# Attention: running sums in 64x64 quadrants of the array, denominators from their own sums of k, their inverses in PSUM

## The chip, the cores and the metric

The kernel runs on one core of a Trainium2 chip. The metric is the device time of one execution in microseconds: 632.59 us is the median of three runs of the kernel before (632.16 to 632.62).

## What is computed

One decoder layer on x of 128 sequences of 64 tokens with 128 features, in float32: causal linear attention with 16 heads of 8 features, a cross attention by autocorrelation, and a mixture of 8 experts. The change touches the linear attention alone:

```python
q = fm(xn @ wq + bq); k = fm(xn @ wk + bk); v = xn @ wv + bv     # fm(a) = a + 1 if a > 0 else exp(a)
# per sequence and head, over the tokens t in order:
S = S + k[:, None] * v[None, :]          # 8 x 8
z = z + k                                # 8
out_t = (q @ S) / ((q . z) + 1e-6)
x = x + out @ wo + bo
```

## The kernel before, in words

The 8192 tokens are 64 tiles of 128 (two sequences of 64 each), in 16 groups of 4 tiles. The attention, and the Gram matrices of the cross attention that follows it, run as a software pipeline of slots, one slot a group: `slot(n)` does stage a0 (statistics and normalisation) of group n+2, a1 (transpose, projection, features, outer products) of group n+1, b (running sums, product with q, sum over d) of group n, c (division, output projection, residual) of group n-1, and d (second normalisation, Gram products) of group n-2. Each engine has its own `slot` function, and the order of its instructions there is the order in which it executes them; semaphores tie the engines. Slots 2 to 13 are in a loop of two slots an iteration, the others are written out.

In one slot, for each tile k of four:

- TensorE projects the normalised, transposed rows to q, k, v (`project`, one 384-column product into bank 1). ScalarE takes the three out (L647, L648, L650, L653); GpSimd adds the two parts of the feature map (L534) and makes the outer product of v and k (L542). v has a ninth column of ones in each head (`v9`, D1 = 9), so that the outer product holds k itself as a ninth row: 16 x 9 x 8 = 1152 columns.
- TensorE multiplies it by a 128x128 block-triangular matrix of ones, `tri_s` (`running_sums`): the running sums over the tokens of each sequence. 1152 columns don't fit one PSUM bank, so there are three products, of 6, 5 and 5 heads, into banks 2, 3 and 4. VectorE multiplies each piece by q (`times_q`, L896), and one reduction sums over d (`sum_heads`, L905) into `nd`, which holds numerators and denominators. As each piece has its own semaphore count, TensorE may refill a bank as soon as its piece of the last tile is multiplied.

In the slot after, ScalarE adds the epsilon to the denominators (L658), VectorE inverts them (`inverses`, L930), and multiplies (`quotients`, L935: both inputs in SBUF). TensorE transposes the quotients (L1333), ScalarE copies them out (L693), TensorE projects them with a bias product, VectorE adds them to X (`add_attention`, L943) and takes the statistics of the sum (L869, L877).

A float32 product is two instructions in the trace, each with its own weight load. All products go through line 1329, all transposes of four tiles through line 1333. The array's order in a slot is: transposes of xh; sums of tile 1; projection 0; the product of `wkk` with the context; projection 1; transposes of the quotients; sums 2; output projection; projection 2; transposes of xh2; sums 3; projection 3; sums of tile 0 of the next group; the Gram products, which are eight 64-column products into the upper and the lower half of the output partitions.

Of the kernel before, what the change touches and what calls it, by code (L numbers as in the profile page):

```python
# [13 lines left out]
P = 128  # L14
B, L, E, H = 128, 64, 128, 16
D = E // H
D1 = D + 1
T = B * L
NT = T // P
GT = 4  # L20
# [33 lines left out]
HEADS = [(0, 6), (6, 11), (11, 16)]  # L54
# [13 lines left out]
def build(nc, x, ctx_t, ctx_r, wqkv_p, b_all, wo, wq2, wk2, wv2t, wo2, bq2, bk2, bv2, scale, w_router, w_experts,  # L68
          tri, stri, ident, iota, dest, walk, place, late_in, out):
    with ExitStack() as ctx:  # L70
        def sb(name, shape, dt=F32):
            return ctx.enter_context(nc.sbuf_tensor(name, shape, dt))

        def sem(name):
            return ctx.enter_context(nc.semaphore(name))

        def sems(name, n):
# [52 lines left out]
        v9 = [sb(f"v9_{i}", [P, H, D1]) for i in range(2)]  # L130
        qk = [sb(f"qk{i}", [P, GT, 2 * E]) for i in range(2)]

        shared = sb("shared", [P, GT * H * D1 * D])
        bias_f, bias_r, bias_a, bias_b = (shared[0:3, i * NBIAS:(i + 1) * NBIAS] for i in range(4))
        b_wide = shared[:, 4 * NBIAS:4 * NBIAS + 3 * E]
        outer = [shared[:, i * H * D1 * D:(i + 1) * H * D1 * D].rearrange("p (h e d) -> p h e d", h=H, e=D1)
                 for i in range(GT)]
        R = sb("R", [P, H, D1, D])
        nd = [sb(f"nd{i}", [P, GT, H, D1]) for i in range(2)]
        den, rden = sb("den", [P, GT * H]), sb("rden", [P, GT * H])  # L140
# [81 lines left out]
        is_tile = [halves(R[:].rearrange("p h e d -> p (h e d)")[:, i * PAIRS * NT:(i + 1) * PAIRS * NT], PAIRS, NT, 2)  # L222
                   for i in range(2)]
        row_t = R[:].rearrange("p h e d -> p (h e d)")[:, NSORT * NT:NSORT * NT + P]
# [13 lines left out]
        bank = [ctx.enter_context(nc.psum_tensor(f"bank{i}", [P, 512], F32)) for i in range(8)]  # L238

# [16 lines left out]
        b_run, b_mul, b_red = sem("b_run"), sem("b_mul"), sem("b_red")  # L256

# [38 lines left out]
        def settle(eng):  # L296


            eng.sem_inc(settled, 1)
# [200 lines left out]
        def _(pool):  # L500
# [5 lines left out]
            for k in range(2):  # L506
                pool.memset(v9[k][:], 1.0).then_inc(setup, 1)
# [5 lines left out]
            pool.wait_ge(setup, 5)  # L513
# [14 lines left out]
            def features(g, p, r, k):  # L528
                t = GT * g + k

                pool.wait_ge(a_ex, t + 1)
                need(pool, b_mul, 3 * (t - 2 * GT) + 3)
                need(pool, a_outer, t - 2 * GT + 1)
                nc.gpsimd.tensor_tensor(qk[p][:, k, :], ex[k % 2][:], rl[k % 2][:], ALU.add).then_inc(a_f, 1)  # L534

            def outer_product(g, p, r, k):
                t = GT * g + k
                pool.wait_ge(a_f, t + 1)
                pool.wait_ge(a_pev, 3 * t + 3)
                need(pool, b_run, 3 * (t - GT) + 3)  # L540
                kk = qk[p][:, k, E:2 * E].rearrange("p (h d) -> p h d", h=H)
                nc.gpsimd.tensor_tensor(  # L542
                    outer[k], v9[k % 2][:].unsqueeze(3).broadcast_to([P, H, D1, D]),
                    kk.unsqueeze(2).broadcast_to([P, H, D1, D]), ALU.mult).then_inc(a_outer, 1)
# [91 lines left out]
        def _(act):  # L636
# [5 lines left out]
            def a_evac_proj(g, p, r, k):  # L642
                t = GT * g + k
                act.wait_ge(a_proj, t + 1)
                need(act, a_f, t - 1)

                nc.scalar.activation(ex[k % 2][:], bank[1][:, 0:2 * E], ACT.Relu, scale=-1.0).then_inc(a_pev, 1)  # L647
                nc.scalar.activation(rl[k % 2][:], bank[1][:, 0:2 * E], ACT.Relu).then_inc(a_pev, 1)  # L648
                need(act, a_outer, t - 1)
                nc.scalar.activation(v9[k % 2][:, :, 0:D], bank[1][:, 2 * E:3 * E].rearrange("p (h d) -> p h d", h=H),  # L650
                                     ACT.Copy).then_inc(a_pev, 1)
                act.wait_ge(a_pev, 3 * t + 1)
                nc.scalar.activation(ex[k % 2][:], ex[k % 2][:], ACT.Exp, scale=-1.0).then_inc(a_ex, 1)  # L653

            def denominators(g, p, r):
                act.wait_ge(b_red, GT * g + GT)
                need(act, c_rden, g)
                nc.scalar.activation(den[:], nd[p][:, :, :, D].rearrange("p t h -> p (t h)"), ACT.Copy, bias=ATT_EPS).then_inc(c_den, 1)  # L658
# [15 lines left out]
            def slot(n, i):  # L674
                a0, a1, c, d = (stage(n, i, s) for s in (2, 1, -1, -2))
# [8 lines left out]
                if c:  # L684
                    denominators(*c)
# [20 lines left out]
                if a1:  # L706
                    a_evac_proj(*a1, 2)
                if a0:
# [118 lines left out]
        def _(dve):  # L827
# [59 lines left out]
            def times_q(g, p, r, k, pieces):  # L887
                t = GT * g + k
                if pieces[0] == 0:
                    need(dve, b_red, t)  # L890
                for c in pieces:
                    lo, hi = HEADS[c]
                    n_h = hi - lo
                    dve.wait_ge(b_run, 3 * t + c + 1)
                    qq = qk[p][:, k, lo * D:hi * D].rearrange("p (h d) -> p h d", h=n_h)
                    nc.vector.tensor_tensor(  # L896
                        R[:, lo:hi], bank[2 + c][:, 0:n_h * D1 * D].rearrange("p (h e d) -> p h e d", h=n_h, e=D1),
                        qq.unsqueeze(2).broadcast_to([P, n_h, D1, D]), ALU.mult).then_inc(b_mul, 1)

            def sum_heads(g, p, r, k):  # L900
                t = GT * g + k
                dve.wait_ge(b_mul, 3 * t + 3)
                if k == 0:
                    need(dve, c_on, g - 1)
                nc.vector.tensor_reduce(nd[p][:, k], R[:], AX.X, ALU.add).then_inc(b_red, 1)  # L905

# [20 lines left out]
            def inverses(g, p, r):  # L927
                dve.wait_ge(c_den, g + 1)
                need(dve, c_on, g)
                nc.vector.reciprocal(rden[:], den[:]).then_inc(c_rden, 1)  # L930

            def quotients(g, p, r):
                dve.wait_ge(c_rden, g + 1)
                need(dve, c_tr, g)
                nc.vector.tensor_tensor(  # L935
                    on[:].rearrange("p t (h d) -> p (t h) d", h=H), nd[p][:, :, :, 0:D].rearrange("p t h d -> p (t h) d"),
                    rden[:].unsqueeze(2).broadcast_to([P, GT * H, D]), ALU.mult).then_inc(c_on, 1)
# [8 lines left out]
            def slot(n, i):  # L946
                a0, a1, b, c = (stage(n, i, s) for s in (2, 1, 0, -1))
                if b:
                    times_q(*b, 0, (0, 1, 2))
                if b:  # L950
                    sum_heads(*b, 0)
                if c:
                    inverses(*c)
                if b:
                    times_q(*b, 1, (0,))
                if c:
                    quotients(*c)
                if b:
                    times_q(*b, 1, (1, 2))
# [4 lines left out]
                if b:  # L964
                    sum_heads(*b, 1)
                if a0:
                    moments(a0[0], a0[1], st_a, a_st, mv_a, a_mv, a_nb, GT)
# [9 lines left out]
                if b:  # L977
                    times_q(*b, 2, (0, 1, 2))
# [7 lines left out]
                if b:  # L986
                    times_q(*b, 3, (0,))
                if c:
                    moments(c[0], c[1], st_c, c_st, mv_c, c_mv, c_nb, GT)
                if b:  # L990
                    times_q(*b, 3, (1, 2))
                    sum_heads(*b, 3)
# [14 lines left out]
            dve.wait_ge(setup, 12)  # L1007
# [319 lines left out]
        def _(pe):  # L1327
# [7 lines left out]

            def running_sums(g, p, r, k):
                t = GT * g + k
                pe.wait_ge(a_outer, t + 1)
                for c, (lo, hi) in enumerate(HEADS):
                    need(pe, b_mul, 3 * (t - 1) + c + 1)  # L1340
                    mm(bank[2 + c][:, 0:(hi - lo) * D1 * D], tri_s[:], outer[k][:, lo:hi].rearrange("p h e d -> p (h e d)")
                       ).then_inc(b_run, 1)

            def project(g, p, r, k):
                t = GT * g + k
                if k == 0:
                    pe.wait_ge(a_xT, g + 1)
                need(pe, a_pev, 3 * t)
                mm(bank[1][:, 0:3 * E], xT[:, k * P:(k + 1) * P], wqkv[:]).then_inc(a_proj, 1)
# [6 lines left out]
            def slot(n, i):  # L1356
# [15 lines left out]
                if b:  # L1372
                    running_sums(*b, 1)
                if a1:
# [12 lines left out]
                if i is None and n == NG:  # L1387
                    pe.wait_ge(b_mul, 3 * NT)
                    keep_warm(2, 10)
                if c:  # L1390
                    pe.wait_ge(c_on, c[0] + 1)
                    transposes(bank[5], on).then_inc(c_tr, 1)
# [47 lines left out]
            pe.wait_ge(setup, 5)  # L1440
# [11 lines left out]
            pe.wait_ge(b_mul, 3 * NT)  # L1452
# [64 lines left out]
            pe.wait_ge(setup, 11)  # L1517
# [196 lines left out]
```

## Time and profile before

| | us |
|---|---|
| median of three runs | 632.59 |
| span of the profiled execution | 631.7 |
| what its run took beyond the span, about | 0.9 |
| first product with q | 21.78 |
| first product with q of group 15 | 252.61 |
| Gram products of group 13 | 263.90 |
| TensorE, VectorE, GpSimd, ScalarE busy | 575.6, 517.9, 427.0, 420.2 |

The attention is the stretch from the first product with q to about 278 us. The second part of the transfer of the Gram diagonals waits for the Gram products of group 13, and everything after it waits for that transfer, so the time at which slot 15 does these products is the end of this stage. Read it slot by slot: a slot is the time from one group's first product with q to the next group's.

### The profile page before, as it was taken

The numbers are of one execution on the slowest core, as the hardware profiler recorded it, in microseconds if no ns is written. First come the engines' busy times: TensorE is split into PE (matmuls) and PEld (weight loads), VectorE is DVE, ScalarE is ACT, GpSimd is POOL, SyncE is SP. The second block draws the span as 40 slices with busy tenths as digits, with TensorE's granted clock in tenths as the row PEclk, the third lists the DMA queues.
The fourth block names the chain that finished last, engine by engine and source line by source line (L and its number), as shares of the span: only waits on it lengthen the run. The fifth ranks groups of instructions, "written<-read, shape, count | busy, mean of one in ns | idle before, by whom it ended". The sixth has DMA issues, their size and how long they took to land.

```text
span 631.7 us, 15833 instructions
## 1 busy us (share of the span) xinstructions
PE 575.6 (91%) x3838; PEld 442.8 (70%) x3839; DVE 517.9 (82%) x1602; ACT 420.2 (67%) x1188; POOL 427.0 (68%) x461
## 2 busy tenths in 40 slices
PE   3899999999999999968799877999999999999993
PEld 1455555555555555545689644799999999989993
DVE  5599999999999999983678888566877887877883
ACT  3557777877787777351788512345788888878882
POOL 2899989998999899310877600765467666757762
PEclk9999999999999999999999968899999999999998
DMA  5610111111161111283477551221012111111110
GB/s 147 184 51 0 35 33 35 34 33 33 33 100 33 34 33 34 66 119 90 119 208 202 113 113 29 53 51 46 27 49 54 48 47 47 51 38 51 51 44 23
DMA packets 49973, 40.92 MB, mean 65 GB/s; under 512 B 21971, under 2 KB 40278, under 8 KB 49926
## 3 DMA queue, kind: packets, MB, share of 16 engines
q1 hardware_dynamic: 44150, 29.61, 19.0%
q0 software_dynamic: 4960, 10.49, 6.4%
q8 instruction: 20, 0.33, 0.2%
q10 hardware_dynamic: 816, 0.26, 0.2%
q14 instruction: 27, 0.22, 0.1%
HBM read 27.47 MB, written 12.88 MB: 64 GB/s over the span
## 4 chain that ended last, share of the span: by engine, by line
PE 63%; ACT 12%; DVE 12%; issue 6%; DMA 4%; POOL 1%; DVEq 0%; ACTq 0%; SPq 0%; POOLq 0%
PE bank L1329 57%; PE bank L1333 4%; ACT xh L671 3%; ACT xs L773 2%; PE bank L1568 2%; DMA w_s<-gram_d 1%; DVE on L935 1%; ACT ex L647 1%; ACT nb_c L668 1%; DVE mean_early L1037 1%; DMA circ<-prob_d 1%; PE bank L1492 1%; ACT rl L648 1%; ACT xrT L759 1%; ACT ex L653 1%
## 5 line engine op out<-in xcount | busy, mean ns | idle before, releaser
L542 POOL TENSOR_TENSOR shared<-v,qk 128x1152 f32<-128x1152 f32 x64 | 142.8, 2231 | 2.8
L1329 PE MATMUL bank<-shared,tri_s 128*128 128x360 f32 (+1 forms) x384 | 137.2, 494 | 0.7 <-DVE R L896 0.7
L609 POOL DMA_INDIRECT shared<-xs_d,row_u x91 | 87.8, 964 | 62.2 <-DVE row_u L1227 31.6
L896 DVE TENSOR_TENSOR R<-bank,qk 128x360 f32<-128x360 f32 (+1 forms) x192 | 96.2, 540 | 8.6 <-PE bank L1329 6.7
L1329 PEld LDWEIGHTS bank<-shared,tri_s 128*128 128x128 f32 x384 | 69.8, 192 | 44.9 <-issue 20.4
L616 POOL DMA_INDIRECT out_x<-shared x64 | 63.6, 993 | 48.4 <-DVE shared L1299 21.8
L905 DVE TENSOR_REDUCE nd<-R 128x144 f32<-128x1152 f32 x64 | 86.1, 1346 | 1.6
L1329 PE MATMUL bank<-w_s,hid 128*128 (+1 forms) x620 | 82.3, 276 | 0.1
L1329 PEld LDWEIGHTS bank<-w_s,hid 128*128 128x128 f32 x620 | 75.5, 192 | 0.6 <-issue 0.3
L812 ACT ACTIVATE shared<-bank 128x256 f32<-128x256 f32 x155 | 59.4, 384 | 21.9 <-PE bank L1329 16.2
L1320 DVE TENSOR_TENSOR hid<-bank,shared 128x256 f32<-128x256 f32 x155 | 61.4, 422 | 10.0 <-ACT shared L812 9.8
L1329 PE MATMUL bank<-shared,ct 128*128 128x128 f32 x512 | 67.8, 275 | 0.0
L1329 PE MATMUL bank<-shared,u 128*128 128x128 f32 x512 | 67.6, 275 | 0.0
L1329 PE MATMUL bank<-wqkv,xT 128*128 128x384 f32 x128 | 56.7, 526 | 6.9 <-ACT v L650 4.6
L1329 PEld LDWEIGHTS bank<-shared,ct 128*128 128x128 f32 x512 | 62.2, 192 | 0.3 <-issue 0.2
L1329 PEld LDWEIGHTS bank<-shared,u 128*128 128x128 f32 x512 | 62.3, 192 | 0.0
L802 ACT ACTIVATE shared<-bank,scale_s 128x128 f32<-128x128 f32 (+1 forms) x78 | 30.1, 386 | 41.1 <-PE bank L1568 41.1
L534 POOL TENSOR_TENSOR qk<-ex,rl 128x256 f32<-128x256 f32 x64 | 48.0, 751 | 9.7 <-ACT ex L653 9.6
L647 ACT ACTIVATE ex<-bank 128x256 f32<-128x256 f32 x64 | 24.1, 376 | 36.2 <-PE bank L1329 36.2
L1329 PEld LDWEIGHTS bank<-wqkv,xT 128*128 128x128 f32 x128 | 22.5, 198 | 29.7 <-ACT v L650 21.6
L806 ACT ACTIVATE ct<-w_s 128x512 f32 x64 | 39.7, 620 | 0.1
L1329 PE MATMUL bank<-ones 128*128 128x512 bf16 x128 | 36.0, 423 | 0.0
(247 smaller groups left out, 1138.4 us busy)
## 6 DMA issues: line engine op xcount, KB each, us to landing
xs_d<-xs SPq DMA_DIRECT2D x16, 270.0 KB, 4.7
X<-in_x SPq DMA_DIRECT2D x16, 256.0 KB, 2.8
ct<-in_ctx_t SPq DMA_DIRECT2D x16, 256.0 KB, 2.8
ct<-in_ctx_r SPq DMA_DIRECT2D x16, 256.0 KB, 3.6
gram_d<-gd SPq DMA_DIRECT2D x14, 256.0 KB, 2.4
w_s<-in_w_experts SPq DMA_DIRECT2D x8, 384.0 KB, 4.0
circ<-prob_d SPq DMA_DIRECT2D x30, 64.0 KB, 2.7
shared<-xs_d,row_u POOLq DMA_INDIRECT x91, 2.6
```

The source lines that it names most:

```text
L534: nc.gpsimd.tensor_tensor(qk[p][:, k, :], ex[k % 2][:], rl[k % 2][:], ALU.add).then_inc(a_f, 1)
L542: nc.gpsimd.tensor_tensor(outer[k], v9[k % 2][:].unsqueeze(3).broadcast_to([P, H, D1, D]), kk.unsqueeze(2).broadcast_to([P, H, D1, D]), AL ...
L609: nc.gpsimd.indirect_dma_start(xg[q], None, xs_d[:, :], bass.IndirectOffsetOnAxis(ap=rows, axis=0)).then_inc(xg_in[q], 16)
L616: nc.gpsimd.indirect_dma_start(out[:, :], bass.IndirectOffsetOnAxis(ap=xg[(NXI + j) % NX][:, DEST:DEST + 1].bitcast(U32), axis=0), yg[q], ...
L647: nc.scalar.activation(ex[k % 2][:], bank[1][:, 0:2 * E], ACT.Relu, scale=-1.0).then_inc(a_pev, 1)
L802: nc.scalar.activation(xgT[p][:, cols], bank[0][:, cols], ACT.Copy, scale=scale_s[:, 0:1]).then_inc(x_xT, 1)
L806: nc.scalar.activation(w_tile[n % 2][0], w_s[:, dyn(held[0] * W_E, 2 * HID)], ACT.Copy).then_inc(x_wa, 1)
L812: nc.scalar.activation(silu[p][h], bank[1 + 2 * p + h][:, HID:2 * HID], ACT.Silu).then_inc(x_silu, 2 // len(items_of(i, up[0])))
L896: nc.vector.tensor_tensor(R[:, lo:hi], bank[2 + c][:, 0:n_h * D1 * D].rearrange("p (h e d) -> p h e d", h=n_h, e=D1), qq.unsqueeze(2).broa ...
L905: nc.vector.tensor_reduce(nd[p][:, k], R[:], AX.X, ALU.add).then_inc(b_red, 1)
L1320: nc.vector.tensor_tensor(hid[p][h][:], bank[1 + 2 * p + h][:, 0:HID], silu[p][h], ALU.mult).then_inc(x_h, 2 // len(items_of(i, j)))
L1329: return nc.tensor.matmul(o, l, r, start=start, stop=stop, skip_group_check=True)
```

## The change

- The ninth column goes: the outer product has 1024 columns (`v8`, `outer`), the running sums fill exactly two banks (`run`, banks 2 and 3), the product with q is one instruction over both, and the reduction gives the 128 numerators alone (`num`).
- `running_sums` becomes four products of 64 rows, 64 output partitions and 512 columns, one for each quadrant of the array: rows of sequence b and head half c give partitions of half c in bank b. So the results lie with the head half in the partition index.
- To have q in that layout, `project` does k and v as one 256-column product and q as four products of 64 output partitions and 64 columns.
- The denominators have a path of their own, once a group: `key_sums`, four products of 64 output partitions and 256 columns (tri_s by the four tiles' k) into bank 4, after the sums of tile 1; `key_dots` times q and `sum_dots` over d on VectorE around the second tile; ScalarE adds the epsilon after the third tile's features; `inverses` comes before the last `sum_heads` of the same slot and writes into bank 4.
- `quotients` comes right after the first product with q of the next slot, with its second input in PSUM.
- `turn_quotients` replaces the four transposes by sixteen products of 64 rows by 64 columns with the identity, on the two diagonal quadrants.
- One semaphore count a tile in place of three; two memsets at the start go.

The core of the diff:

```diff
-            def running_sums(g, p, r, k):
-                for c, (lo, hi) in enumerate(HEADS):
-                    need(pe, b_mul, 3 * (t - 1) + c + 1)
-                    mm(bank[2 + c][:, 0:(hi - lo) * D1 * D], tri_s[:], outer[k][:, lo:hi].rearrange("p h e d -> p (h e d)")
-                       ).then_inc(b_run, 1)
+                need(pe, b_mul, t)
+                settle(pe)
+                for b in range(2):
+                    for c in range(2):
+                        own = slice(b * L, b * L + L)
+                        last = mm(run[c * L:c * L + L, b * 512:b * 512 + 512], tri_s[own, own], outer[k][own, c * 512:c * 512 + 512])
+                last.then_inc(b_run, 1)
+            def turn_quotients():
+                settle(pe)
+                for k in range(GT):
+                    for b in range(2):
+                        for c in range(2):
+                            own = slice(c * HALF, c * HALF + HALF)
+                            last = mm(bank[5][own, k * P + b * HALF:k * P + b * HALF + HALF],
+                                      on[own, k, b * HALF:b * HALF + HALF], id_s[own, own])
+            def key_sums(g, p, r):
+                pe.wait_ge(a_f, GT * g + GT)
+                need(pe, c_on, g)
+                for b in range(2):
+                    for c in range(2):
+                        last = mm(bank[4][c * L:c * L + L, b * GT * HALF:(b + 1) * GT * HALF], tri_s[:, b * L:b * L + L],
+                                  qk[p][:, :, E + c * HALF:E + c * HALF + HALF])
             def project(g, p, r, k):
-                mm(bank[1][:, 0:3 * E], xT[:, k * P:(k + 1) * P], wqkv[:]).then_inc(a_proj, 1)
+                mm(bank[1][:, E:3 * E], xT[:, k * P:(k + 1) * P], wqkv[:, E:3 * E])
+                for b in range(2):
+                    for c in range(2):
+                        last = mm(bank[1][c * L:c * L + L, b * HALF:b * HALF + HALF], xT[:, k * P + b * L:k * P + b * L + L],
+                                  wqkv[:, c * HALF:c * HALF + HALF])
...
+            def times_q(g, p, r, k):
+                need(dve, b_red, t)
+                dve.wait_ge(b_run, t + 1)
+                nc.vector.tensor_tensor(
+                    R[:, 0:D * E].rearrange("p (h e d) -> p h e d", h=H, e=D),
+                    run[:].rearrange("p (h e d) -> p h e d", h=H, e=D),
+                    qq.unsqueeze(2).broadcast_to([P, H, D, D]), ALU.mult).then_inc(b_mul, 1)
+            def key_dots(g, p, r):
+                dve.wait_ge(b_keys, g + 1)
+                nc.vector.tensor_tensor(
+                    zq[:].rearrange("p (k b x) -> p b k x", k=GT, b=2), bank[4][:].rearrange("p (b k x) -> p b k x", b=2, k=GT),
+                    qk[p][:, :, 0:E].rearrange("p k (b x) -> p b k x", b=2), ALU.mult).then_inc(b_dots, 1)
+            def sum_dots(g, p, r):
+                nc.vector.tensor_reduce(den[:], zq[:].rearrange("p (x d) -> p x d", d=D), AX.X, ALU.add).then_inc(b_dots, 1)
```

In VectorE's slot the order before is: `times_q` 0 (three pieces), `sum_heads` 0, `inverses` of group n-1, first piece of `times_q` 1, `quotients` of n-1, its other pieces, statistics of a0, `sum_heads` 1, its moments, `times_q` 2, `add_attention`, `sum_heads` 2, statistics of c, `times_q` 3 around the moments of c, `sum_heads` 3. After: `times_q` 0, `quotients` of n-1, `sum_heads` 0, `times_q` 1, `key_dots`, statistics of a0, `sum_heads` 1, `sum_dots`, moments, `times_q` 2, `add_attention`, `sum_heads` 2, statistics of c, `times_q` 3, moments of c, `inverses` of n, `sum_heads` 3.

## Rows read from the trace of the kernel before

**Rows 1.** The page: busy time of each engine, and the granted clock over the span.
```profile
PE 575.6 (91%) x3838; PEld 442.8 (70%) x3839; DVE 517.9 (82%) x1602; ACT 420.2 (67%) x1188; POOL 427.0 (68%) x461
...
PEclk9999999999999999999999968899999999999998
```

**Rows 2.** Chain of waits, 100 to 160 us: start, us, what.
```profile
123.78 5.13 PE bank L1329 x30
```

**Rows 3.** Timeline of VectorE, 128 to 144 us: start, us, instruction, idle before.
```profile
128.35 1.49 DVE L896 TENSOR_TENSOR R<-bank,qk 128x432 f32<-128x432 f32 x3
129.87 1.35 DVE L905 TENSOR_REDUCE nd<-R 128x144 f32<-128x1152 f32 x1
131.14 0.54 DVE L930 RECIPROCAL rden<-den 128x64 f32<-128x64 f32 x1
...
132.06 0.68 DVE L935 TENSOR_TENSOR on<-nd,rden 128x512 f32<-128x512 f32 x1
...
133.54 0.86 DVE L869 BATCH_NORM_STATS2 st_a<-X 128x6 f32 x4
134.32 1.33 DVE L905 TENSOR_REDUCE nd<-R 128x144 f32<-128x1152 f32 x1
135.57 0.37 DVE L877 BATCH_NORM_AGGREGATE mv_a<-st_a 128x2 f32<-128x6 f32 x4
...
137.71 0.69 DVE L943 TENSOR_TENSOR X<-X,bank 128x512 f32 x1 [0.32 <-PE bank L1329]
...
142.12 1.35 DVE L905 TENSOR_REDUCE nd<-R 128x144 f32<-128x1152 f32 x1
143.60 1.49 DVE L896 TENSOR_TENSOR R<-bank,qk 128x432 f32<-128x432 f32 x3
```

**Rows 4.** Timeline of TensorE, 126 to 135 us.
```profile
126.19 2.10 PE L1329 MATMUL bank<-shared,tri_s 128*128 128x432 f32 x6
128.22 0.69 PE L1329 MATMUL bank<-x2T,k2T 128*64 128x64 f32 x16
128.84 0.66 PE L1333 MATMUL bank<-id_s,xh 128*128 128x128 f32 x4
129.33 2.10 PE L1329 MATMUL bank<-shared,tri_s 128*128 128x432 f32 x6
131.27 0.81 PE L1329 MATMUL bank<-wqkv,xT 128*128 128x384 f32 x2
...
133.07 0.91 PE L1329 MATMUL bank<-wqkv,xT 128*128 128x384 f32 x2
133.82 0.60 PE L1333 MATMUL bank<-id_s,on 128*128 128x128 f32 x4
```

**Rows 5.** Single products of two kinds, 100 to 200 us: ns min/median/max.
```profile
L1333 PE MATMUL bank<-id_s,xh x48: 272/273/329, 107.8 to 191.6; 128*128 128x128 f32 x48
...
L1329 PE MATMUL bank<-x2T,k2T x96: 222/222/271, 113.0 to 191.0; 128*64 128x64 f32 x96
```

**Rows 6.** Timeline of ScalarE, 132 to 139 us.
```profile
132.19 0.38 ACT L647 ACTIVATE ex<-bank 128x256 f32<-128x256 f32 x1 [1.76 <-PE bank L1329]
...
134.46 0.60 ACT L693 ACTIVATE oT<-bank 128x512 f32<-128x512 f32 x1 [1.14 <-PE bank L1333]
...
136.69 1.65 ACT L671 ACTIVATE xh<-X,nb_c,rs_c 128x128 f32 x4
```

**Rows 7.** The quotients (ns min/median/max of 16), and an outer product beside one.
```profile
L935 DVE TENSOR_TENSOR on<-nd,rden x16: 677/679/2592, 40.3 to 268.2; 128x512 f32<-128x512 f32 x16
...
132.11 2.66 POOL L542 TENSOR_TENSOR shared<-v,qk 128x1152 f32<-128x1152 f32 x1
```

**Rows 8.** Timeline of all engines: first and last slot of the running sums.
```profile
21.78 0.61 DVE L896 TENSOR_TENSOR R<-bank,qk 128x432 f32<-128x432 f32 x1 [4.52 <-PE bank L1329]
...
252.61 1.49 DVE L896 TENSOR_TENSOR R<-bank,qk 128x432 f32<-128x432 f32 x3
...
263.90 0.69 PE L1329 MATMUL bank<-x2T,k2T 128*64 128x64 f32 x16
```

More of the change, by code:

```diff
@@ L53 @@
 PITCH = L * (2 * L + 1)
-HEADS = [(0, 6), (6, 11), (11, 16)]
+HALF = E // 2
 def need(eng, sem, count):
@@ L129, in build @@
         ex, rl = [sb(f"ex{i}", [P, 2 * E]) for i in range(2)], [sb(f"rl{i}", [P, 2 * E]) for i in range(2)]
-        v9 = [sb(f"v9_{i}", [P, H, D1]) for i in range(2)]
+        v8 = [sb(f"v8_{i}", [P, E]) for i in range(2)]
         qk = [sb(f"qk{i}", [P, GT, 2 * E]) for i in range(2)]
-        shared = sb("shared", [P, GT * H * D1 * D])
+        shared = sb("shared", [P, 9 * GT * E])
         bias_f, bias_r, bias_a, bias_b = (shared[0:3, i * NBIAS:(i + 1) * NBIAS] for i in range(4))
         b_wide = shared[:, 4 * NBIAS:4 * NBIAS + 3 * E]
[L136 to L140, printed above, removed]
+        outer = [shared[:, i * D * E:(i + 1) * D * E] for i in range(GT)]
+        R = sb("R", [P, (D + 1) * E])
+        num = [sb(f"num{i}", [P, GT, E]) for i in range(2)]
+        zq = sb("zq", [P, GT * E])
+        den = sb("den", [P, GT * H])
         on = sb("on", [P, GT, E])
@@ L236, in build, with psum @@
         y0 = sb("y0", [P, E])
-        bank = [ctx.enter_context(nc.psum_tensor(f"bank{i}", [P, 512], F32)) for i in range(8)]
+        def psum(name, banks=1):
+            return ctx.enter_context(nc.psum_tensor(name, [P, banks * 512], F32))
+        bank = [psum("bank0"), psum("bank1")]
+        run = psum("run", 2)
+        bank += [run[:, i * 512:(i + 1) * 512] for i in range(2)] + [psum(f"bank{i}") for i in range(4, 8)]
+        rden = bank[4][:, 0:GT * H]
         settled = sem("settled")
@@ L531, in features @@
                 pool.wait_ge(a_ex, t + 1)
-                need(pool, b_mul, 3 * (t - 2 * GT) + 3)
+                need(pool, b_mul, t - 2 * GT + 1)
+                need(pool, b_dots, 2 * (g - 1) - 1)
                 need(pool, a_outer, t - 2 * GT + 1)
@@ L539, in outer_product @@
                 pool.wait_ge(a_pev, 3 * t + 3)
-                need(pool, b_run, 3 * (t - GT) + 3)
+                need(pool, b_run, t - GT + 1)
                 kk = qk[p][:, k, E:2 * E].rearrange("p (h d) -> p h d", h=H)
+                vv = v8[k % 2][:].rearrange("p (h e) -> p h e", h=H)
                 nc.gpsimd.tensor_tensor(
-                    outer[k], v9[k % 2][:].unsqueeze(3).broadcast_to([P, H, D1, D]),
-                    kk.unsqueeze(2).broadcast_to([P, H, D1, D]), ALU.mult).then_inc(a_outer, 1)
+                    outer[k].rearrange("p (h e d) -> p h e d", h=H, e=D), vv.unsqueeze(3).broadcast_to([P, H, D, D]),
+                    kk.unsqueeze(2).broadcast_to([P, H, D, D]), ALU.mult).then_inc(a_outer, 1)
             def slot(n, i):
@@ L674, in slot @@
             def slot(n, i):
-                a0, a1, c, d = (stage(n, i, s) for s in (2, 1, -1, -2))
+                a0, a1, b, c, d = (stage(n, i, s) for s in (2, 1, 0, -1, -2))
                 if i is None and n == 1:
@@ L1391, in slot @@
                     pe.wait_ge(c_on, c[0] + 1)
-                    transposes(bank[5], on).then_inc(c_tr, 1)
+                    turn_quotients().then_inc(c_tr, 1)
                 if i is None and n == NG:
```

81 lines of the change are left out of this document (36 added, 45 removed).

## The prediction

> **What bounds the kernel now.** The page comes first: TensorE is busy for 91% of the span at a granted clock of 0.9 or more nearly everywhere, so most of the kernel is the array's [rows 1]. The change works only in the attention, 21.78 to 263.90 us [rows 8], so what counts is how long a slot lasts there. Fifteen slots, from 21.78 to 252.61, take 230.8 us, 15.39 each; an undisturbed one takes 15.25, from 128.35 to 143.60 [rows 3, 8]. Some are longer because of the quotients: the median is 0.68 us, the longest 2.59 [rows 7]. Beside one of them the outer product on GpSimd took 2.66.
>
> Inside a slot no single engine is the bound. VectorE's line is nearly gapless (0.32 us before L943, 0.13 before the next slot [rows 3]). The chain of waits shows runs such as 5.13 us of TensorE [rows 2]; the timelines show how they continue: sums 1, projection 0, ScalarE's copies, projection 1, transposes of the quotients, ScalarE's copy of them, its copies of projection 1, the second normalisation, transposes of xh2 [rows 4, 6]. So the slot is a ring through TensorE and ScalarE, 15.25 us long, and VectorE's own work is just shorter. A change that lightens each engine still has to shorten the longest ring; that is where I work it out.
>
> **How to read TensorE's rows.** Four transposes take 0.60 us and one takes 0.273 [rows 4, 5], so they start 0.109 apart: 0.85 ns a column for each instruction of a product, and 0.164 us of tail that the next one doesn't wait for. The sums of a tile, 1152 columns in two instructions each, are 1.96; the row gives 2.10 - 0.164 = 1.94.
>
> **Quadrants.** The trace before has one tiled shape, the Gram products: sixteen instructions of 64 columns would be 0.87 us one after another; they took 0.69, less 0.164 and 0.05 of slow start 0.47 [rows 4, 5]. So two run at a time in the two column halves. No row shows two row halves together. The bounds of a tile's sums (eight instructions of 512 columns, 0.435 each) are 0.88 us, four at a time, 1.75, two at a time, and 3.5, one by one. I take 0.88, as the Gram rows are at the full rate for their halves: 1.06 less a tile than now. k's sums are eight instructions of 256 columns, two at a time: 0.87 a group. q's projection is 0.23 a tile and the other 256 columns 0.43, together 0.66 against 0.64. The turned quotients are 32 instructions of 64 columns, 0.92 at two at a time against 0.44 now.
>
> **Changing shape.** The sums before the Gram products end streaming at 126.19 + 2.10 - 0.164 = 128.13; the first Gram instruction starts at 128.22 and takes 0.05 longer than the others: 0.14 us lost. On the way back streaming ends at 128.74, the first transpose starts at 128.84 and takes 0.055 longer: 0.155 lost [rows 4, 5]. Between full-size products nothing is lost. I take 0.15 for each change of shape. Before there are two in a slot; after there are sixteen (around each tile's sums, around the q half of each projection, around k's sums, the turned quotients and the Gram products). TensorE's sum in a slot falls by 4 x 1.06 = 4.2, and grows by 0.87 + 0.1 + 0.5 + 14 x 0.15 = 3.6. So the array gains 0.6 us a slot, not four.
>
> The Trainium skill (TensorEngine Tiling (Array Packing), Key Properties) says that changing the tiling mode drains the array, and that changing the tile within a mode doesn't. The trace agrees for full size against column halves; no row here shows quadrants against column halves. By the rule that is a change too; if it were none, two of the six changes in the ring below would go and the result be 0.3 us a slot, some 4 us in all, lower.
>
> **VectorE.** Three products with q take 1.49 us and VectorE's 512-element product from PSUM 0.69 [rows 3]: 1.04 ns an element and 0.15 fixed, 1.22 for 1024 in one. The reduction goes from 1.35 to 1.21. That is 0.41 less a tile, 1.6 a slot. Added are a product of 512 (0.69, next start after 0.61) and a reduction of 512 (0.68, 0.60): 1.2. The inversion keeps its 0.54 (0.46 to the next start), wherever it stands. The quotients keep 0.68 and lose their long cases, as their second input is no longer in SBUF; today's long slots cost 0.14 a slot over the quiet ones. That gain is real, but only where this ring is the bound. Summed in the new order, each from its start to the next start (product with q 1.14, quotients 0.60, reduction 1.13, or 1.34 where a product with q follows it, statistics 0.78, moments 0.29): 14.5 us. By VectorE alone a slot would be 0.7 shorter. GpSimd's outer product shrinks by a ninth, some 0.2 of 2.2 us; it is not in the ring, as it has more than 3 us to spare before the sums that read it. ScalarE's epsilon only moves (0.3), behind the copies of projection 2, before the first normalisation of group n+2, which the next transposes need only 3 us later.
>
> **The new ring.** Two waits get coarser. The sums of tile k now need the whole product with q of tile k-1 (before: its first piece), and the product with q needs the whole sums. So VectorE enters the ring. From the start of the transposes of xh2: 0.50 for them; 0.15 change; sums 3 0.88; 0.22 until VectorE starts (128.13 to 128.35 [rows 3, 4]); product with q 1.14, moments 0.29, inversion 0.46, reduction 1.21 and 0.13 until the next product with q, 3.23; product with q of tile 0 and 0.10 to the array, 1.32; sums 1 0.88; change and k's sums 1.02; change and k, v 0.58; change and q 0.38; ScalarE's copies, 1.27 from the end of projection 0 at 131.91 to the effective start of projection 1 at 133.18 [rows 4, 6] (the context product lies beside this); k, v 0.43; change and q 0.38; change and turned quotients 1.07; and 4.13 from the end of today's transposes at 134.26 to the transposes of xh2 at 138.39 (ScalarE's copy of the quotients, its four copies of projection 1, and the normalisation that ends at 138.34 [rows 6]; the next sums and the output projection lie beside this). Sum 16.44 us. What waits in it: behind the transposes of xh2 stand sums 3, projection 3 and sums 0, and for sums 3 VectorE waits 0.9 us at its fourth product with q. A smaller wait of 0.8 arises at its third, since between sums 1 and sums 2 the array now has five changes of shape.
>
> **The sum.** Slot 0 has neither division nor Gram products; VectorE's 11.9 us and waits make 13.1 (before 14.8). Slot 1 has the division but no second normalisation: 14.5 + 0.8 + 0.1 for `add_attention` = 15.4. Thirteen slots of 16.44 are 213.7. Together 242.2 against 230.8: +11.4. The first product with q needs all the sums of tile 0: +0.3. Slot 15 has no projections; by the same terms its Gram products come 10.1 us after its start, now 11.3: -1.2. In all +10.5. What follows begins with a transfer that waits for those Gram products, and moves with them. The execution's span 631.7 becomes 642.2; with 0.9 beyond the span, which is also how the profiled run stands to the median 632.59, 643 us. The two memsets at the start lie under the first loads: nothing.
>
> **Rivals.**
> - *Faster: VectorE is the ring.* If the array's changes of shape cost little where instructions wait anyway, and the two waits on VectorE are hidden, a slot is VectorE's 14.5 + 0.1. For: it is today's nearly gapless line. Against: 1.8 us of the ring sum have to vanish. 13.1 + 14 x 14.65 = 218.2, -12.6 + 0.3 - 1.2: 619 us. It decides from where the ring falls under 15.2.
> - *Near no change.* The six changes of the ring cost nothing but the ring stands: 16.44 - 0.9 = 15.54, 13 x 0.9 = 11.7 us less than forecast: 631 us.
> - *Slower still: sums two at a time.* The two instructions of one product follow each other in one quadrant; if the second holds up the next quadrant, a tile's sums are 1.75 and the ring 18.2. 13 x 1.75 and 2 for the first slots: 667 us. One by one it would be 3.5 a tile and some 712.
> - *Slower: the turned quotients one at a time*, 1.84 in place of 0.92, 14 times: 656 us. The mechanism is that the two diagonal quadrants have different row halves and write one bank. The Trainium skill (TensorEngine Tiling (Array Packing), Gotcha 1: PSUM Pressure) says that different row tiles can't access one PSUM bank at the same time. No run here shows it.
>
> **Chances.** Forecast and what lies near it (slots of 15.9 to 16.9, 636 to 650) 0.44; faster 0.21; near no change 0.13, of which 0.04 faster, 0.06 within 0.2%, 0.03 slower; two at a time or worse 0.12; turned quotients 0.10. A measurement of this kernel tells 0.2%, 1.3 us, from no change. Faster 0.25, same 0.06, slower 0.69. The range that holds 8 in 10 reaches from the faster case to the two-at-a-time case: 618 to 667; the likeliest alone is 636 to 650.
>
> **What would show it.** Right: slots of about 16.4 us with VectorE idle before its third and fourth product with q, released by L1329; 0.15 of idle weight loads at each change of shape; a tile's eight instructions within 0.9 us; all sixteen quotients at 0.68. Wrong: no idle time on VectorE (faster); the eight instructions over 1.7 us; a granted clock under 0.9 within the attention, as TensorE's share of a slot falls to about 13.8 of 16.4 us (which I count with nothing, since by the ring it never stands still for longer than about 1.2 us).

## The result, and the profile after

The changed kernel takes 646.54 us (median of 4 runs, 646.11 to 647.40); the kernel before took 632.54 beside it (4 runs). The ratio is 1.0217 [1.0202, 1.0231]: 14.0 us slower. The profiled execution has a span of 645.6 and a time of 647.4. Forecast were 643 us, 618 to 667.

The page of the changed kernel: span, then busy time of each engine, the granted clock in 40 slices, and who holds the chain that ends last [rows 1].

```profile
span 645.6 us, 18065 instructions
...
PE 562.5 (87%) x5054; PEld 419.2 (65%) x5055; DVE 504.7 (78%) x1506; ACT 417.8 (65%) x1188; POOL 410.0 (64%) x459
...
PEclk9999999999999999999999977899999999999997
...
PE 59%; ACT 14%; DVE 11%; issue 8%; DMA 3%; POOL 2%; ACTq 0%; DVEq 0%; POOLq 0%; SPq 0%
```

Every engine is lighter (TensorE by 13 us, VectorE by 13, GpSimd by 17, ScalarE by 2) and the kernel is longer. TensorE's granted clock is as before (in both traces it is on record as 1.00 from 25 to 366 us, so in nearly all of the attention). That is what a ring does: each engine has slack, and the way round them has grown.

The same stretch of two engines, one slot. Columns: start, us, instruction, idle before and what ended it. VectorE first [rows 3]:

```profile
132.45 1.23 DVE L897 TENSOR_TENSOR R<-run,qk 128x1024 f32<-128x1024 f32 x1 [0.97 <-PE run L1342]
133.59 0.37 DVE L882 BATCH_NORM_AGGREGATE mv_c<-st_c 128x2 f32<-128x6 f32 x4
133.87 0.53 DVE L945 RECIPROCAL bank<-den 128x64 f32<-128x64 f32 x1
134.31 1.17 DVE L907 TENSOR_REDUCE num<-R 128x128 f32<-128x1024 f32 x1
135.59 1.23 DVE L897 TENSOR_TENSOR R<-run,qk 128x1024 f32<-128x1024 f32 x1
136.74 0.68 DVE L951 TENSOR_TENSOR on<-num,bank 128x512 f32<-128x512 f32 x1
...
144.14 1.23 DVE L897 TENSOR_TENSOR R<-run,qk 128x1024 f32<-128x1024 f32 x1 [0.88 <-PE run L1342]
```

TensorE [rows 4]:

```profile
130.70 0.66 PE L1346 MATMUL bank<-id_s,xh 128*128 128x128 f32 x4 [1.16 <-ACT xh L676]
131.29 1.09 PE L1342 MATMUL run<-shared,tri_s 64*64 64x512 f32 x8
...
135.79 0.66 PE L1346 MATMUL bank<-id_s,xh 128*128 128x128 f32 x4 [0.31 <-ACT xh L676]
136.92 1.09 PE L1342 MATMUL run<-shared,tri_s 64*64 64x512 f32 x8 [0.47 <-issue]
137.94 1.08 PE L1342 MATMUL bank<-qk,tri_s 128*64 128x256 f32 x8
138.96 1.08 PE L1342 MATMUL bank<-wqkv,xT 128*128 128x256 f32 x10
139.97 1.13 PE L1342 MATMUL bank<-ct,wkk 128*128 128x512 f32 x2
141.04 1.08 PE L1342 MATMUL bank<-wqkv,xT 128*128 128x256 f32 x10
142.05 1.08 PE L1342 MATMUL bank<-id_s,on 64*64 64x64 f32 x29
142.92 0.64 PE L1342 MATMUL run<-shared,tri_s 64*64 64x512 f32 x1
...
143.03 1.03 PE L1342 MATMUL run<-shared,tri_s 64*64 64x512 f32 x6
...
147.18 0.66 PE L1346 MATMUL bank<-id_s,xh 128*128 128x128 f32 x4 [1.09 <-ACT xh L676]
```

Read them as one way round. From transposes of xh2 to transposes of xh2 it is 147.18 - 130.70 = 16.48 us. VectorE stands still twice, before its fourth (0.97) and its third (0.88) product with q, both times until TensorE's sums. TensorE stands still 1.1 us before the transposes of xh2 in each slot, until ScalarE's second normalisation. Before, VectorE had 0.32 and 0.13.

A tile's eight quadrant instructions take 0.93 us (136.92 to 137.85, which is 1.09 less the 0.164 of tail), where the full-size ones took 1.94. So the array does what was asked of it. The rows that pay for it are the short ones around: k's sums, a projection in two shapes (1.01 us from start to next start; one shape took 0.64), turned quotients (0.87 until the next sums begin; four transposes had 0.44).

Where the 14 us lie, from first product with q to first product with q:

| | forecast | measured | before |
|---|---|---|---|
| first product with q of tile 0 | 22.1 | 23.34 | 21.78 |
| slot 0 | 13.1 | 13.20 | 14.80 |
| slot 1 | 15.4 | 16.55 | 14.74 |
| slots 2 to 14, mean | 16.44 | 16.50 | 15.48 |
| Gram products of group 13, after slot 15 starts | 10.1 | 10.14 | 11.29 |
| they start at | 274.4 | 277.68 | 263.90 |

The last row has grown by 13.8 us and the span by 13.9, so all that follows the attention only moved.

### The profile page after: what moved, and what is told of

Same layout as the page of the kernel before. It is cut to its first block, busy times and chain, and to the rows that moved or that the text cites. A ratio compares the mean times of both kernels' runs of the same rounds, so it can differ in the third digit from the quotient of the medians.

```text
span 645.6 us, 18065 instructions
## 1 busy us (share of the span) xinstructions
PE 562.5 (87%) x5054; PEld 419.2 (65%) x5055; DVE 504.7 (78%) x1506; ACT 417.8 (65%) x1188; POOL 410.0 (64%) x459
## 4 chain that ended last, share of the span: by engine, by line
PE 59%; ACT 14%; DVE 11%; issue 8%; DMA 3%; POOL 2%; ACTq 0%; DVEq 0%; POOLq 0%; SPq 0%
PE bank L1342 38%; PE run L1342 16%; ACT xh L676 4%; PE bank L1346 3%; ACT xs L778 2%; PE bank L1611 2%; ACT ex L654 2%; DMA w_s<-gram_d 1%; ACT nb_c L673 1%; ACT ex L659 1%; DVE mean_early L1050 1%; DVE R L897 1%; DVE num L907 1%; PE run L1535 1%; ACT nb_a L673 1%
## 5 line engine op out<-in xcount | busy, mean ns | idle before, releaser
L549 POOL TENSOR_TENSOR shared<-v,qk 128x1024 f32<-128x1024 f32 x64 | 125.1, 1955 | 2.8
L897 DVE TENSOR_TENSOR R<-run,qk 128x1024 f32<-128x1024 f32 x64 | 78.4, 1224 | 38.4 <-PE run L1342 35.4
L1342 PEld LDWEIGHTS bank<-wqkv,xT 128*64 128x64 f32 (+1 forms) x640 | 40.8, 152 | 63.7 <-ACT v L657 34.3
L1342 PE MATMUL run<-shared,tri_s 64*64 64x512 f32 x512 | 71.3, 618 | 10.6 <-issue 7.9
L1342 PE MATMUL bank<-wqkv,xT 128*64 128x64 f32 (+1 forms) x640 | 70.8, 279 | 10.5 <-ACT v L657 9.7
L907 DVE TENSOR_REDUCE num<-R 128x128 f32<-128x1024 f32 x64 | 76.6, 1198 | 0.1
L1346 PE MATMUL bank<-id_s,xh 128*128 128x128 f32 x128 | 21.7, 294 | 22.1 <-ACT xh L676 22.0
L1333 DVE TENSOR_TENSOR hid<-run,shared 128x256 f32<-128x256 f32 x78 | 33.0, 423 | 8.0 <-ACT shared L817 7.8
L1342 PE MATMUL bank<-shared,ct 128*128 128x128 f32 x256 | 34.0, 276 | 0.0
L1342 PE MATMUL run<-shared,ct 128*128 128x128 f32 x256 | 33.9, 275 | 0.1
L1342 PE MATMUL run<-shared,u 128*128 128x128 f32 x256 | 33.8, 275 | 0.0
```

The lines of the kernel that those rows point to most:

```text
L549: nc.gpsimd.tensor_tensor(outer[k].rearrange("p (h e d) -> p h e d", h=H, e=D), vv.unsqueeze(3).broadcast_to([P, H, D, D]), kk.unsqueeze(2 ...
L897: nc.vector.tensor_tensor(R[:, 0:D * E].rearrange("p (h e d) -> p h e d", h=H, e=D), run[:].rearrange("p (h e d) -> p h e d", h=H, e=D), q ...
L907: nc.vector.tensor_reduce(num[p][:, k, :], R[:, 0:D * E].rearrange("p (x d) -> p x d", d=D), AX.X, ALU.add).then_inc(b_red, 1)
L1333: nc.vector.tensor_tensor(hid[p][h][:], bank[1 + 2 * p + h][:, 0:HID], silu[p][h], ALU.mult).then_inc(x_h, 2 // len(items_of(i, j)))
L1342: return nc.tensor.matmul(o, l, r, start=start, stop=stop, skip_group_check=True)
L1346: last = nc.tensor.transpose(o[:, k * P:(k + 1) * P], src[:, k, :], id_s[:])
```

## The experiments

Ratios are to the kernel before, run beside each. "Slot" is a slot in the steady middle of the attention, read from VectorE's products with q.

**How many run at a time.** The running sums on column halves alone, with all 128 rows:

```diff
-  last = mm(run[c * L:c * L + L, b * 512:b * 512 + 512], tri_s[own, own], outer[k][own, c * 512:c * 512 + 512])
+  last = mm(run[c * L:c * L + L, b * 512:b * 512 + 512], tri_s[:, own], outer[k][:, c * 512:c * 512 + 512])
```

> The changed kernel, with the running sums in column halves only: each product has all 128 rows (the other sequence's rows of tri_s are zero), 64 output partitions and 512 columns. Theory (ring): the eight instructions go two at a time, 1.75 us a tile in place of 0.88; sums 1 and sums 3 stand in the ring, so a slot goes from 16.5 to 18.2 and the time up by 14 x 1.75 = 24, to about 671. Rival (the four sums of a tile lie beside VectorE's work, and what lengthened the slot is the changes of shape alone): under 5 us more.

Measured: 675.48 us, 1.0672 [1.0636, 1.0707], slots of 18.15 to 18.27. TensorE's timeline in it:

```profile
131.92 1.94 PE L1342 MATMUL run<-shared,tri_s 128*64 128x512 f32 x8 [0.36 <-DVE R L897]
133.66 1.06 PE L1342 MATMUL bank<-qk,tri_s 128*64 128x256 f32 x8
```

1.74 from start to next start, at the same shape as what follows (with quadrants 1.02, a change of shape included). Quadrants run four at a time, column halves two. The ring holds two tiles' sums, and the slot grew by 1.7, twice the 0.85 by which each row is longer (1.94 and 1.09). Two small terms lie beside that and about cancel: one change of shape fewer, and sums 0, which now hold VectorE's next product with q for 0.27. Four at a time is real and is worth 29 us here against two; the changed kernel would be much worse without it.

**The ring's ScalarE arc.** The second normalisation ahead of ScalarE's wait for the turned quotients; all else as changed:

```diff
 if d:
     g, p, r = d
     need(act, d_tr, g)
     norm(g, p, rs_c, c_rs, ..., xh2, d_xh, ...)
 ...  # ScalarE's copy of the turned quotients and of projection 1, formerly ahead of it
```

> The changed kernel; ScalarE does the second normalisation before it waits for the turned quotients, not after it has copied them and projection 1. Nothing is removed on any engine. Theory (ring through ScalarE): its 4.15 us between the turned quotients and the transposes of xh2 become TensorE's own work there (sums 2 0.9, change and output projection 1.24, waits, projection 2 0.8, change), the transposes of xh2 start about 0.9 us earlier, the slot is 15.5 and the time about 633. Rival (VectorE's own line or TensorE's sum is the bound): no change, 646 to 647.

Measured: 632.59 us, 0.9994 [0.9972, 1.0016], slots of 15.57 to 15.62. One position in ScalarE's order takes back the whole loss. TensorE no longer waits for that normalisation:

```profile
139.90 0.98 PE L1342 MATMUL bank<-wqkv,xT 128*128 128x256 f32 x10
140.81 0.66 PE L1346 MATMUL bank<-id_s,xh 128*128 128x128 f32 x4
```

Slot 1, which has no second normalisation, kept its 16.52.

**The inversion.** It stands between the fourth product with q and the reduction, so that the next product with q waits for it. Moved ahead of the fourth product, where VectorE was idle (ScalarE's epsilon moved ahead too, so that it is there in time):

```diff
+ inverses(*b)          # ahead of times_q 3
  times_q(..., 3)
- inverses(*b)          # ahead of sum_heads 3
```

> The changed kernel; the inversion goes before the fourth product with q, where VectorE waits 0.97 us, and ScalarE's epsilon before its copy of x2T. Theory (ring): 0.46 us less between the fourth product with q and the next slot, slot 16.05, time 640.5. Rival (that stretch of VectorE is covered by projection 3 and sums 0, which lie beside it): no change, 646.

Measured: 642.05 us, 1.0150 [1.0111, 1.0189], slots of 16.14 to 16.23: 0.35 less a slot. The idle time before the fourth product fell from 0.97 to 0.43, as the inversion (0.55) now fills it:

```profile
145.61 0.55 DVE L946 RECIPROCAL bank<-den 128x64 f32<-128x64 f32 x1
146.59 1.22 DVE L898 TENSOR_TENSOR R<-run,qk 128x1024 f32<-128x1024 f32 x1 [0.43 <-PE run L1343]
```

**The changes of shape.** The k, v part of each projection, and the context product, in column halves as well, so that they follow the q part, k's sums and each other with no change:

```diff
-  mm(bank[1][:, E:3 * E], xT[:, k * P:(k + 1) * P], wqkv[:, E:3 * E])
+  for b in range(2):
+      mm(bank[1][b * L:b * L + L, E:3 * E], xT[:, k * P + b * L:k * P + b * L + L], wqkv[:, E:3 * E])
...
-  mm(bank[7][:], wkk[:, 0:E], ct[p][:]).then_inc(d_k, 1)
+  for h in range(2):
+      last = mm(bank[7][h * L:h * L + L, :], wkk[:, h * L:h * L + L], ct[p][:])
```

> The changed kernel; projection of k and v, and the product with the context, as two products each for the two output halves. Same columns times instructions over two halves, so the same streaming time; but the array no longer changes shape between k's sums, projection, q half and context product. Theory (each change 0.15 us, three of them in the ring: before k and v of projection 0, before both q halves): 0.45 us a slot, 6 us, about 640. Rival (a change costs only where the next instruction's wait would not have hidden it, or halves run slower than full size): 0 to 2 us, or slower.

Measured: 638.14 us, 1.0073 [1.0046, 1.0100], slots of 15.92 to 16.05: 0.54 less. More instructions, the same columns streamed, 8.4 us gained (9.1 by the two ratios). The first slots gained too: the first product with q came at 21.89 in place of 23.34. TensorE at the start of the changed kernel and then of this one:

```profile
16.74 1.84 PE L1342 MATMUL bank<-wqkv,xT 128*128 128x256 f32 x10 [0.93 <-ACT v L657]
19.51 1.85 PE L1342 MATMUL bank<-wqkv,xT 128*128 128x256 f32 x10 [0.93 <-ACT v L657]
```

```profile
16.07 1.55 PE L1342 MATMUL bank<-wqkv,xT 128*64 128x256 f32 x12 [0.93 <-ACT v L657]
18.54 1.55 PE L1342 MATMUL bank<-wqkv,xT 128*64 128x256 f32 x12 [0.93 <-ACT v L657]
```

**The denominators off the ring.** k's sums stand between sums 1 and projection 0, both on the ring. Here they come after projection 2, before TensorE waits for the normalisation, `key_dots` fills VectorE's wait before its fourth product with q, and sum, epsilon and inversion go to the next slot:

```diff
 # TensorE
-   key_sums(*b)        # after sums 1
+   key_sums(*b)        # after projection 2, before the transposes of xh2
 # VectorE
-   quotients(*c); sum_heads 0; times_q 1; key_dots(*b)
+   sum_dots(*c); sum_heads 0; inverses(*c); times_q 1; quotients(*c)
-   sum_dots(*b)        # after sum_heads 1
+   key_dots(*b)        # before times_q 3
-   inverses(*b)        # before sum_heads 3
 # ScalarE
-   denominators(*b)    # after the third tile's features
+   denominators(*c)    # first in the next slot
```

> The changed kernel; k's sums stand before the transposes of xh2, where the array waits 1.1 us for ScalarE, the product with them before the fourth product with q, where VectorE waits 0.97, and their reduction, epsilon and inversion in the next slot. Theory (ring): 1.02 of k's sums and 0.46 of the inversion leave the ring, slot 14.95 to 15.1, time 625. Rival (VectorE's own work bounds from 15 us on, or k's sums delay the transposes of xh2): slot 15.3 to 15.6, time 630 to 635.

Measured: 628.55 us, 0.9931 [0.9914, 0.9947], slots of 15.20: 0.1 to 0.25 above what the ring's terms gave. The trace has a likely reason for 0.15 of it, which no run tests: with k's sums gone, projection 0 starts 1.17 us after sums 1 (126.81 to 127.98) where k's sums had started after 1.02, and 0.13 after ScalarE's copy of the transposed rows that it reads has ended (127.85). It is 0.13 in every steady slot, where the changed kernel has 1.25 or more, so that copy is now what projection 0 waits for. Slot 1 fell from 16.55 to 14.40.

With the column halves as well:

> keys_late with the projection of k and v and the context product in output halves. Theory (ring): two more changes of shape leave it, 0.3 us a slot, slot 14.65 to 14.8, time about 621. Rival (VectorE's 14.4 to 14.5 and its waits bound already): the same as keys_late within 1.5 us.

Measured: 621.33 us, 0.9809 [0.9792, 0.9825], slots of 14.85, the Gram products of group 13 at 252.62. This is the best version, 12 us under the kernel before that ran beside it (633.40) and 25 under the changed one. VectorE in it:

```profile
133.97 0.68 DVE L913 TENSOR_TENSOR zq<-bank,qk 128x512 f32<-128x512 f32 x1
134.94 1.22 DVE L897 TENSOR_TENSOR R<-run,qk 128x1024 f32<-128x1024 f32 x1 [0.29 <-PE run L1345]
136.08 0.37 DVE L882 BATCH_NORM_AGGREGATE mv_c<-st_c 128x2 f32<-128x6 f32 x4
136.37 1.18 DVE L907 TENSOR_REDUCE num<-R 128x128 f32<-128x1024 f32 x1
137.68 1.23 DVE L897 TENSOR_TENSOR R<-run,qk 128x1024 f32<-128x1024 f32 x1
```

0.29 of idle time in a slot is left. The forecast's sum of VectorE's own work was 14.5, and 14.86 - 0.29 is 14.57: VectorE is now all but the bound, which is what the change could have had. TensorE still waits 0.21 us for ScalarE's second normalisation.

With the early normalisation on top, the three cures together:

> keys_late_halves with the second normalisation early. Theory: the ring through ScalarE was 14.65 and VectorE's own line is 14.4 to 14.5, so at most 0.2 us a slot is left: 618 to 621. Rival (VectorE's line has become the bound before): no change against keys_late_halves; or slower, as the copy of the quotients now waits for the normalisation.

Measured: 622.85 us, 0.9833 [0.9817, 0.9849], slots of 14.80. No gain: the slots are 0.05 shorter, but the Gram products of group 13 come 12.63 after slot 15 starts, not 11.04. There the granted clock fell to the lower of its two levels (1.2 GHz), from 246.10 to 249.51 us. Stretches of 6 us around it (busy time, then the granted clock in the column before the last two), first in this kernel, then in the one without the early normalisation:

```profile
244.00:250.00 6.00, 4.18 (x45) 2.57 (x46) 3.39 (x4) 3.13 (x9) 1.41 (x1) 0.72 0.12 40
```

```profile
243.00:249.00 6.00, 4.16 (x53) 1.68 (x54) 4.85 (x7) 1.32 (x6) 3.44 (x3) 1.00 0.30 90
```

TensorE had stood still for 0.94 and 1.84 us just before in the one, 0.95 and 1.84 in the other. So the idle time does not tell them apart, and why one fell to the lower level is left open, as is whether the kernel's other runs had it. The profiled run shows the price: a tile's sums there took 1.98 in place of 1.09.

**The inverses in PSUM alone.** The kernel before, only with its inverse denominators in a free PSUM bank:

```diff
-  den, rden = sb("den", [P, GT * H]), sb("rden", [P, GT * H])
+  den = sb("den", [P, GT * H])
+  rden = bank[5][:, 0:GT * H]
```

> The kernel before, with one thing changed: the inverses of the denominators lie in PSUM (bank 5) and not in SBUF. Theory (the quotients' long cases are VectorE and GpSimd waiting for each other on SBUF when VectorE reads two SBUF inputs): all sixteen quotients take 0.68 us, the three slots of 16.7 become 15.2, time 628. Rival (the long cases come from something else, such as the loop's instruction loads, or lie beside the ring through TensorE and ScalarE): 632.5.

Measured: 628.52 us, 0.9925 [0.9909, 0.9942]. All sixteen quotients take 0.67 to 0.69 us (before up to 2.59 [rows 7]), and the three slots of 16.7 are gone: 15.25 to 15.30 in the middle. The kernel before also shows when a quotient is long. Its three longest (from 85.12, 147.40 and 209.74 us) start 0.14 to 0.18 us after an outer product on GpSimd has started, and end 0.5 us after that product's end. Where the quotient starts first, it keeps its 0.68, and the outer product takes up to 2.71 in place of 2.18. The other way round, the changed kernel with its inverses in SBUF again:

```diff
+  rden = sb("rden", [P, GT * H])[:]
-  rden = bank[4][:, 0:GT * H]
```

> The changed kernel with the inverses in SBUF again. In its trace the quotients run from 136.74 to 137.42 and GpSimd's features of the fourth tile from 136.98, and k's sums start 0.2 us after those features end. Theory (VectorE with two SBUF inputs and GpSimd wait for each other): the features start 0.4 later, k's sums with them, and as these are in the ring a slot gets 0.2 to 0.4 longer: 649 to 651. Rival (the collision needs the long outer product, which stands elsewhere in this order): 646.5, all quotients at 0.68 as now.

Measured: 648.91 us, 1.0255 [1.0224, 1.0287], 2.4 above the changed kernel's median; the two intervals just overlap and the profiled spans differ by 1.0 only, so the traces have to say it. Only two quotients are long (up to 2.31 us). The steady slots are 16.58 to 16.67 (16.47 to 16.59), the Gram products of group 13 start 1.35 later, and GpSimd shows why. In this kernel, VectorE's quotients, GpSimd's last feature addition, and k's sums that read it:

```profile
137.29 0.68 DVE L951 TENSOR_TENSOR on<-num,rden 128x512 f32<-128x512 f32 x1
```

```profile
137.52 1.04 POOL L540 TENSOR_TENSOR qk<-ex,rl 128x256 f32<-128x256 f32 x1 [0.59 <-DVE R L897]
```

```profile
138.61 1.08 PE L1342 MATMUL bank<-qk,tri_s 128*64 128x256 f32 x8
```

In the changed kernel the same addition took 0.73, and k's sums came 2.35 us after the first product with q, not 2.46:

```profile
136.98 0.73 POOL L540 TENSOR_TENSOR qk<-ex,rl 128x256 f32<-128x256 f32 x1 [0.60 <-DVE R L897]
```

So it can be the GpSimd side that pays, while the quotients keep their 0.68. The Trainium skill (SBUF — State Buffer, SBUF: two separate sides) says that VectorE, when an instruction has two inputs in SBUF, and GpSimd share a pair of ports under an exclusive lock. The traces agree that one holds up the other, with 0.31 on GpSimd here and up to 1.9 on VectorE before.

**The old kernel with the good parts that need no quadrants**: inverses in PSUM and the normalisation early.

> The kernel before with the inverses in PSUM (bank 5) and the second normalisation before ScalarE's wait for the transposed quotients. Theory (with finer waits, VectorE's own line bounds there right behind the ring through ScalarE): slots 15.0 in place of 15.27, time 624 to 626. Rival (ScalarE's part is covered in this kernel, its VectorE line with its waits is the bound): 628.5, as without it.

Measured: 625.88 us, 0.9885 [0.9856, 0.9914], slots of 15.04 to 15.06 (15.25 to 15.30 without the move). The move is worth 0.2 a slot where VectorE is nearly gapless, and 0.9 in the changed kernel. It is 4.6 us behind the best version, whose slots of 14.85 it can't reach, as VectorE's own work in the old layout fills 15.0.

## Why the forecast came out

The direction, the mechanism and most terms held; the total was 3.5 us low. That the ring is right to 0.04 is in part luck, as two misses of 0.09 cancel. Term by term, from transposes of xh2 at 130.70:

| term | forecast | measured |
|---|---|---|
| transposes, change, sums 3, start of VectorE | 1.75 | 1.75 (to 132.45) |
| product with q, moments, inversion, reduction, next product | 3.23 | 3.14 |
| product with q of tile 0, to sums 1 | 1.32 | 1.33 |
| sums 1, change and k's sums, k, v and q of projection 0 | 2.86 | 2.95 (to 139.87) |
| ScalarE's copies | 1.27 | 1.28 |
| projection 1, turned quotients | 1.88 | 1.88 (to 143.03) |
| to the transposes of xh2 | 4.13 | 4.15 |
| ring | 16.44 | 16.48 |

- **Quadrants.** Four at a time was taken over two at a time although no row showed two row halves together: a guess that held (0.93 less the tail, for 0.88; column halves 1.74). That rival was worth 29 us, measured, and would have been 667 by the forecast; 675 is what it is.
- **Changes of shape.** 0.15 each was from two rows. Splitting the k, v part takes three of them out of the ring and gained 0.54 a slot, 0.18 each if the changes are all that this run took away. The Trainium skill (TensorEngine Tiling (Array Packing), Key Properties) has the array drain at a change of mode and not at a change of tile; the rows here agree for quadrants against column halves as well: the streaming of sums 1 ends at 137.85, and k's sums begin at 137.94 and need 1.02 until the next row for the 0.87 that they stream. Turned quotients and the sums after them, both quadrants, even overlap: sums 2 begin at 142.92, 0.11 before they have the array to themselves (143.03).
- **Turned quotients.** Two at a time, into one bank, as forecast: 32 instructions from 142.05 to 143.03. The rival of one at a time (1.84), for which the Trainium skill (TensorEngine Tiling (Array Packing), Gotcha 1: PSUM Pressure) spoke, is out: 32 instructions of 64 columns in 0.98 us are two at a time, so two row halves wrote one bank together, each to partitions of its own.
- **"If the ring falls under 15.2, VectorE decides"** was the faster rival's condition. Its mechanism is right, its condition wasn't met by the change, and is met once the ring is shortened: slots of 14.85.
- **What failed: the first slots.** Three terms carry the 3.3 us. The first product with q was put 0.3 later and came 1.56 later. I priced that stretch by rows from the steady state, and only its last wait, for all the sums of tile 0 (0.36 of the 1.56). Another 0.24 is there before the first projection starts, as the first product waits that much longer for its load. The other 0.96 are the four projections, each with a change of shape inside, and the change before the sums: 0.20 a projection (its row takes 1.85 there, before the change 1.65). They were put at nothing. The run with the column halves, which has two changes there in place of eight, had its first product with q 1.45 earlier again. Nor do steady rows hold there. The sums of tile 0 and of tile 1 in the changed kernel:

```profile
21.29 1.99 PE L1342 MATMUL run<-shared,tri_s 64*64 64x512 f32 x8
...
24.91 1.09 PE L1342 MATMUL run<-shared,tri_s 64*64 64x512 f32 x8
```

  And a tile's sums (six of the eight instructions) in the stretch of the three cures together whose granted clock is recorded at the lower level:

```profile
247.31 1.98 PE L1345 MATMUL run<-shared,tri_s 64*64 64x512 f32 x6
```

  For 12 to 23 us the profile gives a granted clock of 1.00, but its clock records begin only at 24.65 us. By its rows TensorE is at the lower level (1.2 GHz) until then, in the kernel before as well (a tile's sums 4.05 us from 20.09, later 2.10).

  Slot 1 was put at 15.4 and took 16.55, and the change's new wait that I had left out is the reason. k's sums need the features of all four tiles of a group, so GpSimd's addition for the fourth tile:

```profile
39.43 0.73 POOL L540 TENSOR_TENSOR qk<-ex,rl 128x256 f32<-128x256 f32 x1
40.21 1.08 PE L1342 MATMUL bank<-qk,tri_s 128*64 128x256 f32 x8 [1.23 <-POOL qk L540]
46.40 1.22 DVE L897 TENSOR_TENSOR R<-run,qk 128x1024 f32<-128x1024 f32 x1 [1.59 <-PE run L1342]
```

  39.43 + 0.73 is 40.16, and TensorE goes on 0.05 later, having stood still for 1.23, with projections 0 and 1 and sums 2 queued behind it. In the steady slots the addition ends 0.2 before the array would be there, which is why it is seen in slot 1 alone, and why slowing it by 0.31 came through as 0.1 in every slot. Moving k's sums away took slot 1 to 14.40. Thirteen slots at 16.50 rather than 16.44 are the last 0.8.
- **The inverses in PSUM** were called a real gain where this ring is the bound. Measured: 4.9 us on the kernel before, 2.4 in the changed one. So the other parts of the change cost 18 us (646.5 against the old kernel's 628.5 with that part alone). Moving the normalisation takes back 14 of them; moving k's sums and the inversion, with the normalisation where it was, takes back all 18 (628.55). Such gains don't add up: they shorten one ring, until VectorE's own line decides.
- **Not tested.** The coarser waits (one semaphore count a tile in place of three) bring VectorE into the ring. Their terms fit the trace, but no run has the quadrants with finer waits, so their share of the loss is worked out and not measured.

## What to carry to other kernels

In a pipeline of engines, sum the longest way round the engines before counting what each one saves: here three engines were lighter by 13 us or more, the fourth by 2, and the kernel 14 slower, and moving one stage, ScalarE's second normalisation, ahead of a wait took the loss back. Small products in several shapes should be ordered or split so that neighbours have one shape; the split costs nothing in columns, and a change of shape cost 0.15 to 0.18 us here. Work that is wanted only a slot later belongs where its engine waits anyway, and what it reads must be looked up first, as a product on the sums of four tiles waits for the last of four.

## What was not expected of the hardware

- The two instructions of a float32 product, in four quadrants, are issued in fours: the first four of a tile start 0.007 us apart (136.922 to 136.942), the second four 0.45 to 0.48 us later.
- TensorE's rows at the start are those of the lower clock level (a tile's sums 1.99 us, later 1.09), while the profile, which has no clock record there, shows 1.00. A change of shape within a projection adds 0.20 us there.
- Two kernels with the same idle time of TensorE (0.95 and 1.84 us) ran on, one at a granted clock of 1.00, the other from 246.10 to 249.51 us at the lower level.
- A quotient on VectorE with both inputs in SBUF, itself at its usual 0.68 us, made an addition on GpSimd beside it take 1.04 in place of 0.73.
